# A layer norm bias folded through the weight signs: summed by GpSimd and two matmuls with ones, in place of four matmuls and an exchange by DMA

## The reference, cut to what matters

```python
    def _L0_ffn_ref(x, weight, gamma, beta, ln_weight, ln_bias):
        mean = jnp.mean(x, axis=-1, keepdims=True)
        var = jnp.mean(jnp.square(x - mean), axis=-1, keepdims=True)
        xn = (x - mean) * jax.lax.rsqrt(var + EPS) * ln_weight + ln_bias
        quant_w = jnp.sign(weight)
        scale = jnp.max(jnp.abs(weight))
        out = jnp.einsum('bsk,ok->bso', xn, quant_w)
        return out * scale * gamma + beta
    x = x + jnp.tanh(g_xattn[0]) * _L0_xattn_ref(_layernorm(x, axis=-1), ctx_1024, L0_xattn_Wq, L0_xattn_bq, L0_xattn_Wk, L0_xattn_bk)
    x = x + jnp.tanh(g_ffn[0]) * _L0_ffn_ref(_layernorm(x, axis=-1), L0_ffn_weight, L0_ffn_gamma, L0_ffn_beta, L0_ffn_ln_weight, L0_ffn_ln_bias)
```

## Time and profile before

| | us |
|---|---|
| median of 3 runs | 123.22 (123.19 to 123.69) |
| the profiled execution | 123.26 |
| its span, first to last instruction | 121.5 |
| TensorE busy | 117.3 (97%) |
| GpSimd busy | 95.6 (79%) |
| VectorE busy | 94.6 (78%) |
| ScalarE busy | 85.8 (71%) |

### The profile page before, as it was taken

The page is one execution under the profiler, slowest core; times in us unless marked ns, Lnnn a source line. Parts: engine busy times, 40 slices in busy tenths (PEclk is TensorE's granted clock), DMA queues, the critical chain, the costliest instruction groups (busy, mean ns, idle before and its releaser), DMA issues.

```text
span 121.5 us, 1890 instructions
## 1 busy us (share of the span) xinstructions
PE 117.3 (97%) x566; PEld 95.1 (78%) x566; DVE 94.6 (78%) x188; ACT 85.8 (71%) x183; POOL 95.6 (79%) x109
## 2 busy tenths in 40 slices
PE   7999999999999999999999999999999999999980
PEld 6578888888888888878889888878898888888870
DVE  0159989997987995699967982998859948989991
ACT  3455899999997979376999794469997972245200
POOL 2049999939068998999986999994748999999970
PEclk9999999999999999999999999999999999999999
DMA  3999898741653410027771302547000012220045
GB/s 107 325 323 365 323 393 300 262 148 54 149 183 103 132 41 5 3 90 269 271 233 20 153 5 86 171 175 245 14 0 3 3 74 105 86 86 0 0 163 183
DMA packets 10109, 17.15 MB, mean 141 GB/s; under 512 B 1522, under 2 KB 2036, under 8 KB 10100
## 3 DMA queue, kind: packets, MB, share of 16 engines
q1 hardware_dynamic: 9808, 16.78, 40.1%
q10 hardware_dynamic: 292, 0.26, 0.7%
HBM read 12.59 MB, written 4.19 MB: 138 GB/s over the span
## 4 chain that ended last, share of the span: by engine, by line
PE 96%; DVE 2%; issue 0%
PE ps_y L428 37%; PE ps_ffn L441 23%; PE ps_score L363 7%; PE ps_turn L395 6%; PE ps_score L395 3%; PE ps_score L518 3%; PE ps_y L395 3%; PE ps_y L386 2%; PE ps_turn L327 2%; PE ps_ffn L386 2%; PE ps_ffn L342 2%; PE ps_score L372 1%; PE ps_turn L363 1%; PE ps_y L510 1%; PE ps_ffn L457 1%; PE ps_ffn L351 1%
## 5 line engine op out<-in xcount | busy, mean ns | idle before, releaser
L926 POOL TENSOR_TENSOR xt_lo<-xt_raw,xt_hi 128x512 fp32r<-128x512 f32 x16 | 22.0, 1377 | 5.4 <-ACT xt_hi L569 3.2
L428 PE MATMUL ps_y<-pt_hi,xt_hi 128*128 128x512 f32 x64 | 18.0, 403 | 0.0
L428 PE MATMUL ps_y<-pt_hi,xt_lo 128*128 128x512 f32 x64 | 17.5, 395 | 0.0
L428 PE MATMUL ps_y<-pt_lo,xt_hi 128*128 128x512 f32 x64 | 17.5, 395 | 0.0
L441 PE MATMUL ps_ffn<-w_sign,zt_hi 128*128 128x512 f32 x60 | 17.2, 409 | 0.0
L557 ACT ACTIVATE prob<-ps_score,neg_max 128x512 f32<-128x512 f32 x14 | 9.5, 680 | 10.2 <-DVE neg_max L705 10.2
L441 PE MATMUL ps_ffn<-w_sign,zt_lo 128*128 128x512 f32 x60 | 16.5, 396 | 0.0
L428 PEld LDWEIGHTS ps_y<-pt_lo,xt_hi 128*128 128x128 f32 x64 | 12.0, 188 | 2.9
L428 PEld LDWEIGHTS ps_y<-pt_hi,xt_lo 128*128 128x128 f32 x64 | 12.0, 188 | 2.9
L772 DVE SCALAR_TENSOR_TENSOR ffn<-ps_ffn,rstd,gain 128x512 f32<-128x512 f32 x14 | 10.4, 744 | 4.4 <-PE ps_ffn L441 2.7
L428 PEld LDWEIGHTS ps_y<-pt_hi,xt_hi 128*128 128x128 f32 x64 | 11.7, 189 | 2.4
(11 more groups left out here) (186 smaller groups left out, 270.9 us busy)
## 6 DMA issues: line engine op xcount, KB each, us to landing
xt_raw<-in_x_t_dram SPq DMA_DIRECT2D x16, 256.0 KB, 2.9
ctx_sb<-in_ctx_t_dram SPq DMA_DIRECT2D x8, 256.0 KB, 5.0
x_sb<-in_x_dram SPq DMA_DIRECT2D x8, 256.0 KB, 4.7
ctx_sb<-in_x_dram SPq DMA_DIRECT2D x8, 256.0 KB, 5.8
out_dram<-x SPq DMA_DIRECT2D x8, 256.0 KB, 2.0
out_dram<-ctx_sb SPq DMA_DIRECT2D x7, 256.0 KB, 2.0
w_raw<-in_weight_t_dram SPq DMA_DIRECT2D x4, 256.0 KB, 7.5
ln_w<-in_ln_weight_dram SPq DMA_DIRECT2D x1, 256.0 KB, 5.4
```

Of the source, the lines that this page charges most:

```text
L428: mm = pe.matmul(ps_y[t % 2][:, :], lhs[:, t, k, :], rhs[:, k, :], start=(k == 0 and i == 0), stop=(k == KN - 1 and i == 2))
L926: nc.gpsimd.tensor_tensor(xt_lo[:, t, :, :], xt_raw[:, t, :, :], xt_hi[:, t, :, :].bitcast(f32), ALU.subtract).then_inc(xt_lo_done, 1)
```

## The change

The sum over k is split in two. GpSimd multiplies each row block of `w_sign` by its column of `lnb_col` (`weigh`, one value for each partition) and adds the four products: `shift_h` and `lnb_part`, seven operations, each waiting for the one before but for the first two. The result is split in a rounded part and a rest, `lnb_sum`. Two matmuls with a tile of ones then sum over the partitions and leave the whole row in all 128 of them, so that no exchange is needed. `sum_bias` moves behind `attend(0, 3)`, where it waits for `lnb_sum` and for VectorE's reading of `ps_ffn[0]`. VectorE, no longer ScalarE, evicts, and multiplies by `gain` on the way. On ScalarE, Sign is moved ahead of three of the four `bias_x`. On GpSimd, the splits of tiles 2 and 3 of batch 0 stand behind the first two `weigh`, `power2(0, 0)` behind the last `add_part`, and in the first `back` the split of batch 1, tile 0 and the addition into `shift` stand ahead of `add_shift(0, 0)`, and `scale_x(1)` ahead of `add_shift(0, 1)`.

```diff
@@ sync
             load_next(0, 0)
-            sp.wait_ge(ffn_evac, 1)
-            for to, frm in ((slice(0, P // 2), slice(P // 2, P)), (slice(P // 2, P), slice(0, P // 2))):
-                sp.dma_start(h_swap[to, :], shift_h[frm, :]).then_inc(swap_in, 16)
             for t in range(1, T):
@@ tensor: feed
                 pe.wait_ge(zt_hi_done, T * b + t + 1)
-                pe.wait_ge(ffn_evac, T * b + max(t, 1))
-                if is_first(b) and t == 1:
-                    pe.wait_ge(scale_done, 1)
+                if t > 0 or not is_first(b):
+                    pe.wait_ge(ffn_evac, T * b + max(t, 1))
+                if is_first(b) and t == 0:
+                    pe.wait_ge(sign_done, 1)
@@ tensor: spread_max, sum_bias
                 pe.wait_ge(wmax_done, KN + 1)
-                pe.wait_ge(ffn_evac, 1)
...
-                pe.wait_ge(sign_done, 1)
+                pe.wait_ge(ones_done, 2)
                 pe.wait_ge(lnb_done, 2)
-                for k in range(KN):
-                    mm = pe.matmul(ps_ffn[0][:, :], lnb[:, k, :], w_sign[:, k, :],
-                                   start=(k == 0), stop=(k == KN - 1))
-                mm.then_inc(ffn_ready, 1)
+                pe.wait_ge(scale_done, 1)
+                for i in range(2):
+                    mm = pe.matmul(ps_ffn[0][:, :], ones_r[:, :], lnb_sum[:, i, :], start=(i == 0), stop=(i == 1))
+                mm.then_inc(bias_summed, 1)
@@ tensor: back
                 attend(b, 1)
-                if is_first(b):
-                    sum_bias()
                 scores(b + 1, 1)
@@
                 attend(b, 3)
+                if is_first(b):
+                    sum_bias()
                 turn_ffn(b, 2)
@@ scalar
-                if is_first(b):
-                    act.wait_ge(ffn_ready, 1)
-                    nc.scalar.activation(shift_h[:, :], ps_ffn[0][:, :], ACT.Copy).then_inc(ffn_evac, 1)
@@
-            bias_x(0, range(T))
+            bias_x(0, range(1))
             for k in range(KN):
                 act.wait_ge(w_in[k], 16)
             nc.scalar.activation(w_sign[:, :, :], w_raw[:, :, :], ACT.Sign).then_inc(sign_done, 1)
+            bias_x(0, range(1, T))
@@ vector: back
                 add_y(b, 3)
                 mean_x1(b, 3)
+                if is_first(b):
+                    dve.wait_ge(gain_done, 1)
+                    dve.wait_ge(bias_summed, 1)
+                    nc.vector.tensor_tensor(shift_h[:, :], ps_ffn[0][:, :], gain[:, :], ALU.mult).then_inc(ffn_evac, 1)
                 stats_x(b + 1, (3,))
@@ gpsimd: back
-                add_shift(b, 0)
-                add_shift(b, 1)
-                if b > 0:
+                if is_first(b):
+                    split_xt(b + 1, 0)
+                    pool.wait_ge(ffn_evac, 1)
+                    pool.wait_ge(shift_done, 1)
+                    nc.gpsimd.tensor_tensor(shift[:, :], shift[:, :], shift_h[:, :], ALU.add).then_inc(shift_done, 1)
+                    pool.wait_ge(shift_done, 2)
+                    add_shift(b, 0)
+                    scale_x(b + 1)
+                    add_shift(b, 1)
+                else:
+                    add_shift(b, 0)
+                    add_shift(b, 1)
                     power2(b, 0)
-                split_xt(b + 1, 0)
-                scale_x(b + 1)
+                    split_xt(b + 1, 0)
+                    scale_x(b + 1)
                 add_shift(b, 2)
@@ gpsimd: ahead of the loop over the batches
+            nc.gpsimd.memset(ones[:, :], 1.0).then_inc(ones_done, 1)
+            pool.wait_ge(ones_done, 1)
+            nc.gpsimd.tensor_copy(ones_r[:, :], ones[:, :]).then_inc(ones_done, 1)
             pool.wait_ge(gates_in, 16 * 3)
-            nc.gpsimd.tensor_copy(lnb[:, :, :P // 2], lnb_col[:, :].unsqueeze(2).broadcast_to([P, KN, P // 2]))\
-                     .then_inc(lnb_done, 1)
-            pool.wait_ge(lnb_done, 1)
-            nc.gpsimd.tensor_tensor(lnb[:, :, P // 2:], lnb_col[:, :].unsqueeze(2).broadcast_to([P, KN, P // 2]),
-                                    lnb[:, :, :P // 2].bitcast(f32), ALU.subtract).then_inc(lnb_done, 1)
+            pool.wait_ge(sign_done, 1)
+
+            def weigh(dst, k):
+                nc.gpsimd.tensor_scalar(dst[:, :], w_sign[:, k, :].bitcast(f32), lnb_col[:, k:k + 1], 1.0,
+                                        ALU.mult, ALU.mult).then_inc(part_done, 1)
+
+            def add_part(count):
+                pool.wait_ge(part_done, count)
+                nc.gpsimd.tensor_tensor(shift_h[:, :], shift_h[:, :], lnb_part[:, :], ALU.add).then_inc(part_done, 1)
+
+            weigh(shift_h, 0)
+            weigh(lnb_part, 1)
             for t in range(HALF, T):
                 split_xt(0, t)
+            add_part(2)
+            pool.wait_ge(part_done, 3)
+            weigh(lnb_part, 2)
+            add_part(4)
+            pool.wait_ge(part_done, 5)
+            weigh(lnb_part, 3)
+            add_part(6)
+            power2(0, 0)
+            pool.wait_ge(part_done, 7)
+            nc.gpsimd.tensor_copy(lnb_sum[:, 0, :], shift_h[:, :]).then_inc(lnb_done, 1)
+            pool.wait_ge(lnb_done, 1)
+            nc.gpsimd.tensor_tensor(lnb_sum[:, 1, :], shift_h[:, :], lnb_sum[:, 0, :].bitcast(f32), ALU.subtract)\
+                     .then_inc(lnb_done, 1)
             pool.wait_ge(rows_in, 48)
             nc.gpsimd.tensor_scalar(shift[:, :], shift[:, :], tanh_g[:, 1:2], 1.0, ALU.mult, ALU.mult)\
                      .then_inc(shift_done, 1)
-            pool.wait_ge(ffn_evac, 1)
-            pool.wait_ge(swap_in, 32)
-            nc.gpsimd.tensor_tensor(shift_h[:, :], shift_h[:, :], h_swap[:, :], ALU.add).then_inc(shift_done, 1)
-            power2(0, 0)
-            pool.wait_ge(gain_done, 1)
-            pool.wait_ge(shift_done, 2)
-            nc.gpsimd.tensor_tensor(shift_h[:, :], shift_h[:, :], gain[:, :], ALU.mult).then_inc(shift_done, 1)
-            pool.wait_ge(shift_done, 3)
-            nc.gpsimd.tensor_tensor(shift[:, :], shift[:, :], shift_h[:, :], ALU.add).then_inc(shift_done, 1)
-            pool.wait_ge(shift_done, 4)
```

More of the change, by code:

```diff
@@ L61, in flamingo_block_kernel @@
         shift_h = sb("shift_h", [P, N])
-        h_swap = sb("h_swap", [P, N])
+        lnb_part = sb("lnb_part", [P, N])
+        lnb_sum = sb("lnb_sum", [P, 2, N], f32r)
+        ones = sb("ones", [P, P])
+        ones_r = sb("ones_r", [P, P], f32r)
         lnb_col = sb("lnb_col", [P, KN])
-        lnb = sb("lnb", [P, KN, P], f32r)
         gates = sb("gates", [P, 2])
@@ L134, in flamingo_block_kernel @@
         rows_in = sem("rows_in")
-        swap_in = sem("swap_in")
         table_done = sem("table_done")
@@ L148, in flamingo_block_kernel @@
         lnb_done = sem("lnb_done")
+        part_done = sem("part_done")
+        ones_done = sem("ones_done")
+        bias_summed = sem("bias_summed")
         gain_done = sem("gain_done")
@@ L762, in scale_ffn @@
             def scale_ffn(b, t):
-                dve.wait_ge(ffn_ready, 1 + T * b + t + 1)
+                dve.wait_ge(ffn_ready, T * b + t + 1)
                 if b == 0 and t == 0:
@@ L859, in last @@
                 turned_ffn_lo(b, 2)
-                dve.wait_ge(ffn_ready, 1 + T * b + 2)
+                dve.wait_ge(ffn_ready, T * b + 2)
                 scale_in_place(b, 1, ps_ffn[0], slice(0, N))
@@ L868, in last @@
                 for h, cols in enumerate(halves):
-                    dve.wait_ge(ffn_ready, 1 + T * b + t + 1 + h)
+                    dve.wait_ge(ffn_ready, T * b + t + 1 + h)
                     scale_in_place(b, t, half_bank[h], cols)
```

## The result

The changed kernel takes 125.11 us (median of 4 runs, 124.83 to 125.47) where the kernel before takes 123.31: a ratio of 1.0145 with a 95% interval of 1.0111 to 1.018, slower by 1.8 us. A second measurement, of 6 executions, gave 125.30 against 123.49, 1.0144 (1.0104 to 1.0185). The forecast was 124.9, 123.3 to 125.8. The profiled execution took 125.47 us, with a span of 123.7.

The account below looks back on a forecast made before the run. TensorE was taken as the path from first matmul to last, with GpSimd close beside it. 123.26 - 0.47 (matmuls) + 1.6 (first wait) + 0.5 (rest of the second wait) = 124.9 us, range 123.3 to 125.8.

Parts of the forecast that it names:

- TensorE is the path: TensorE, busy 117.3 of 121.5 us, bounds the kernel; work elsewhere counts only once it makes TensorE wait.
- The saved matmuls: On TensorE, sum_bias goes from four matmuls (0.93 us) to two (0.46), a gain of 0.47 us.
- The first wait: TensorE waits at the moved sum_bias from 37.87 until GpSimd's sum is ready at 39.45: 1.6 us (0.8 at least).
- `gain`: VectorE's multiplication of gain meets a GpSimd addition in the sum's chain and delays GpSimd: 0 to 0.45, taken as 0.33 us.
- The second wait: TensorE waits again at the load of xt_lo of batch 1, tile 2, leaving 1.65 us later than before; adds 0.5 us.
- GpSimd goes on: After the sum at 39.45 GpSimd's steps follow without idle time, so xt_lo of (1, 1) starts 1.73 us late.
- (a): Only the wait at sum_bias counts, GpSimd's backlog being taken in before 55 us: 123.4 to 124.3 us; chance 0.16.
- (b): GpSimd's sum is ready before TensorE's load at 37.87, so sum_bias is hidden: 122.8 or 122.6 us; chance 0.11.
- (c): TensorE's clock falls to its lower level after the new stops, 2 to 4 us for a spell: 126.5 to 129; chance 0.03.
- (d): A third TensorE wait at zw or feed(0, 1) in the first round, up to 0.8 more: 125.3 to 126; chance 0.08.
- The engines priced at nothing: SP's queue, ScalarE's new order and VectorE's multiply with its wait were priced at 0; VectorE up to 0.5 in the upper end.

Follow-up runs that it names:

- the kernel with the early sum: Changed kernel with one of four row blocks summed, power2(0, 0) behind the chain, sum_bias ahead of attend(0, 3), earlier VectorE multiply, GpSimd reordered: 122.96 us.
- The extra operation in the kernel before: Kernel before plus one unread 128x512 GpSimd multiplication (1.30 us) behind scale_x in the first back: 124.71 us, ratio 1.0103.
- the early split: Changed kernel with GpSimd's split of batch 1, tile 2 ahead of add_ffn of tile 1 in the first back: 124.32 us, 1.0074 to the kernel before.
- sum later on TensorE: Changed kernel with sum_bias 1.3 us later on TensorE, behind turn_ffn of tile 2 and two turn_prob: 124.81 us, 1.0101 to the kernel before.
- cut sum: Changed kernel with GpSimd summing only the first of four row blocks, three weigh and three add_part left out: 124.33 us, 1.0058 to the kernel before.
- cut sum, power behind: Changed kernel summing one of four row blocks, with power2(0, 0) also moved behind the whole chain on GpSimd: 124.06 us, 1.0054 to the kernel before.
- whole sum, shorter chain: Changed kernel, whole sum, first add_part ahead of the two splits of batch 0 and power2(0, 0) behind the chain: 124.94 us, 1.0125.
- the last version: Changed kernel, whole sum: first add_part and split of (1, 2) earlier, power2(0, 0) behind the chain, ScalarE's split of (1, 0) ahead of one exponential: 123.41 us.

## Why the prediction was right, point by point

**The total.** The forecast's rise was 1.6 us. The medians give 1.8 (1.4 to 2.2 by the interval), the profiles 1.4 from the mark to the end.

**TensorE is the path; a loss elsewhere counts only as its wait.** Right. Its matmuls are 564 instead of 566, and the two waits stand in its row as the only low slices.

**The saved matmuls, 0.47.** Right: the two that stay take 0.47 of the 0.93 in the chain of the kernel with the early sum, and that kernel, in which no matmul waits, is 0.47 us shorter from the mark to the end. The second figure is of one execution each.

**The first wait, 1.6.** Right: 1.62, in both profiles. The chain was forecast to end at 39.45; it ended at 40.16, with the mark 0.79 later, so at 39.37. Within it `gain` cost 0.15 and not 0.33, since VectorE came to it only 0.16 before GpSimd's addition ended, and the cast lost 0.49 to `centre`.

**The second wait.** Right in place, releaser and size. The forecast had GpSimd 1.73 late at the split of (1, 1) and TensorE 1.65 late behind the wait; counted from the mark they are 51.08 - 24.84 - (48.72 - 24.05) = 1.57 and 57.87 - 24.84 - (55.57 - 24.05) = 1.51. The extra operation in the kernel before shows that there is next to no slack, and the early split shows that the wait is worth 0.8 to 1.0.

That GpSimd alone times TensorE from there on shows in six profiles. In each the load waits for the split of (1, 2), and the span ends the same time behind the end of that split. The last column is GpSimd's own time, from the start of Sign to that end; where Sign stands in the order of the kernel before, it isn't comparable and is left out.

| kernel | split of (1, 2) ends | span | difference | from Sign |
|---|---|---|---|---|
| changed | 57.82 | 123.7 | 65.9 | 34.29 |
| sum later on TensorE | 57.23 | 123.1 | 65.9 | 34.30 |
| before, one operation more | 57.00 | 122.8 | 65.8 | |
| cut sum | 57.06 | 122.9 | 65.8 | 33.58 |
| cut sum, power behind | 55.62 | 121.5 | 65.9 | 33.58 |
| whole sum, shorter chain | 57.12 | 122.9 | 65.8 | 33.73 |

**The step that was incomplete.** The forecast charged the second wait to the chain's length: "GpSimd goes on" from 39.45, step after step. The steps are right, but they hid a second bound. With six microseconds of the chain cut away, the split still ended 0.88 us later than before, counted from the mark, and not earlier. The part that the forecast passed over is the sum's move behind `attend(0, 3)`: the row is evicted at 40.7, so neither the addition into `shift` nor an `add_shift` can run sooner, and the split put ahead of them waits 0.98 us for ScalarE. The change costs about 1.8 us; with the cut sum it costs 0.7 to 0.9, and with the cut sum made early nothing (0.4 less than before, within the noise). So taking the length away is worth 0.8 to 1.0 by the medians (0.7 by the profiles), and then moving the place, with the order around it, 1.1. That is one order of taking away; as the two are bounds of which the later one counts, they need not add up otherwise. The whole sum with an early place was not tried: by its rows the chain would be ready only behind `attend(0, 3)` and TensorE would wait for it longer. The total came out because in the changed kernel the chain is the later of the two, by little: the multiply ends at 41.76, having waited for the chain itself, and GpSimd comes to the addition at 42.03.

**The first stall can't be fixed alone.** This followed from the forecast's own equation, in which TensorE's lateness at the second wait is GpSimd's lateness and not the sum of the waits. Two kernels that reduce the first wait from 1.62 to 0.56 or 0 stay at 124.8 and 124.9, neither clear of 125.3.

**The rivals.** (a), only the first wait: refuted by the row at 57.87 and by the early split. (b), the sum in time: refuted by 1.62 us (the forecast's argument against it counted three of four additions of 1.30; with all, the eight steps alone are 7.9, still under the 8.2 at which it decides, and only the gaps and meetings lift the chain over it); with a cut and early sum it is what happens, 122.96. (c), the clock: granted in full at both waits; a lone 8 in the last slice is behind the last matmuls. (d), a third wait: none in the changed kernel that the kernel before hasn't too, but it is what came up in the repaired ones (`zw`, `feed`), and perhaps why they stop at parity, which no run shows.

**The engines priced at nothing.** SP's transfers, ScalarE's reordering and VectorE's new wait (0.97 us idle ahead of the multiply) cost nothing that TensorE felt.

## What to carry to other kernels

An engine at 79% busy can have next to no slack at the one place that counts. Before giving it work, find the next load of the bound engine that it feeds, and subtract its end from that load's start: here one operation of 1.30 us cost 1.3. And ask of a moved step both how long its chain is and when its result can first be used: with six microseconds of the chain gone, nearly half of the loss was still there.

## What the runs showed of the hardware that I had not expected

A `centre` of VectorE (two inputs) that a large operation of GpSimd held ended 0.53 to 0.56 us behind it, in all twelve profiles, as in the earlier trace rows. Where `centre` started in the last 0.1 us of one such operation, as at 52.41 there, GpSimd's next went ahead of it too. A power of two columns did not hold it like that. Twice in the changed kernel:

```profile
37.58 0.75 DVE L745 SCALAR_TENSOR_TENSOR zw<-x,neg_mean,ln_w 128x512 f32<-128x512 f32 x1
...
89.08 0.71 POOL L985 TENSOR_TENSOR rstd<-var,neg_half 128x2 f32<-128x2 f32 x1
89.53 0.73 DVE L745 SCALAR_TENSOR_TENSOR zw<-x,neg_mean,ln_w 128x512 f32<-128x512 f32 x1
```

The first started beside the power that ran until 37.74 and took 0.75, as when it is alone. The second started 0.26 before its power's end and ended 0.47 behind it, sooner than behind any large operation. It is GpSimd's cast behind the first power that was held: it started at 37.70, took 1.10 instead of 0.61 and ended 0.47 behind `centre`. The Trainium skill, SBUF — State Buffer, SBUF: two separate sides, says that the first of the two to start holds the pair of ports for its whole instruction. The trace agrees for `centre` and the cast; for the powers, which also started first, it doesn't.

The multiplication by `gain` is held as well. In the last version it started at 36.52, within 0.03 us of GpSimd's subtraction, and took 1.61 us instead of 0.55, ending 0.29 behind it. In the changed kernel it met only the last 0.16 us of an addition and took its 0.55.

And the start of the program isn't the same twice: the same prologue put the mark at 24.05 in the kernel before and between 23.35 and 24.84 in the others, with the difference already there at the projections behind the first loads, which start between 10.4 and 11.9 us. The two profiles of the cut sum with the late place have marks 1.44 apart (24.79 and 23.35) and times 1.44 apart (124.75 and 123.31). Over 1 us of spread in single runs can come with it, so a difference under some 0.35 us (the half width of the interval of most comparisons here, 0.3%) could not be settled.
